# Edge rows turned behind the last tile, layer 0's sums cleared by ScalarE, packed words unpacked the other way round

## The reference

```
x = LN(x + relu(GAT(x)))            # layer 0: 8 heads, softmax over the edges of a node
x = LN(x + two GCN convolutions)    # layer 1: 256 -> 512 -> 256, degree norms, layer norms, relu
x = LN(x + relu(segsum((x@W)[src] * edge_weight, dst) + b))          # layer 2
m = (x@Wf.T)[src]*attr0 + (x@Wr.T)[src]*attr1                        # layer 3: 4 heads
x = LN(x + segsum(softmax(leaky(m@a.T)) * m, dst))
```

## Time and profile before

| | before |
|---|---|
| device time, median of 3 runs | 6573.53 us (6570.21 to 6581.08) |
| span of the profiled execution, first to last instruction | 5313.9 us |
| mean granted TensorE clock | 0.820 |
| busy: PE, DVE, ACT, POOL | 74%, 66%, 48%, 73% |

### The profile page before, as it was taken

How to read it: one execution, slowest core, us unless ns; L and a number is a source line. 1 busy time by engine, 2 the same in 40 slices (tenths; PEclk the granted TensorE clock), 3 DMA queues, 4 the chain that set the end, 5 groups by cost and what they waited for, 6 DMA issues and landing times.

```text
span 5313.9 us, 86764 instructions
## 1 busy us (share of the span) xinstructions
PE 3931.6 (74%) x13357; PEld 2389.2 (45%) x13357; DVE 3517.2 (66%) x10780; ACT 2554.6 (48%) x6938; POOL 3875.0 (73%) x3995
## 2 busy tenths in 40 slices
PE   6888888887777777677777777777677656666763
PEld 4666666664444444344444443343333333444442
DVE  6789888885554545444444445666666578888887
ACT  1667667664555555455545552000000166666665
POOL 3777777775777777677777776777777677777775
PEclk8889889988899998887777777877888777777776
DMA  5444444443333333443333333333333322222222
GB/s 151 113 122 126 122 126 124 120 121 98 111 112 112 111 112 111 118 139 111 111 112 112 111 112 100 109 109 109 109 108 109 98 57 57 57 57 57 57 57 68
DMA packets 252628, 549.14 MB, mean 103 GB/s; under 512 B 71467, under 2 KB 136235, under 8 KB 252108
## 3 DMA queue, kind: packets, MB, share of 16 engines
q0 software_dynamic: 178752, 478.34, 32.8%
q1 hardware_dynamic: 66972, 58.64, 3.5%
q10 hardware_dynamic: 6384, 6.62, 0.5%
HBM read 501.16 MB, written 42.15 MB: 102 GB/s over the span
## 4 chain that ended last, share of the span: by engine, by line
PE 32%; POOL 22%; DMA 18%; issue 13%; DVE 6%; ACT 6%; SPq 2%; DVEq 1%; ACTq 0%; POOLq 0%
PE bank L1453 18%; POOL scratch L1863 12%; DMA scratch<-tab_x,src_idx 10%; POOL scratch L1399 9%; DMA scratch<-tab_h,src_idx 7%; PE bank L1297 4%; PE bank L172 4%; PE bank L1154 3%; DVE reg_acc L1463 2%; ACT scratch L1066 2%; POOL reg_x L1024 2%; SPq L865 1%; DVE reg_acc L1322 1%; PE bank L1142 1%; PE bank L157 1%
## 5 line engine op out<-in xcount | busy, mean ns | idle before, releaser
L1453 PE MATMUL bank<-scratch 128*128 x4986 | 1946.5, 501 | 739.9 <-SPq L1414 356.6
L1463 DVE TENSOR_TENSOR reg_acc<-reg_acc,bank 128x256 f32 x2493 | 1047.3, 420 | 1368.2 <-PE bank L1453 1310.3
L1399 POOL DMA_INDIRECT scratch<-tab_x,src_idx x1566 | 1494.3, 954 | 533.5 <-issue 259.4
L1453 PEld LDWEIGHTS bank<-scratch 128*128 128x128 f32 x4986 | 961.2, 229 | 1630.2 <-issue 1582.6
L1024 POOL DMA_INDIRECT reg_x<-tab_h,src_idx x832 | 838.7, 1008 | 302.7 <-issue 184.1
L1399 POOL DMA_INDIRECT scratch<-tab_h,src_idx x783 | 746.6, 953 | 264.7 <-issue 153.0
L1863 POOL DMA_INDIRECT scratch<-tab_h,src_idx x783 | 743.0, 949 | 249.3 <-issue 226.8
L1916 PE MATMUL bank<-reg_w,scratch 128*128 128x260 f32 x1664 | 639.8, 527 | 282.7 <-issue 180.1
L1423 ACT ACTIVATE scratch<-iota_row,dst_loc 128x128 f32<-128x128 f32 x1662 | 579.6, 393 | 345.5 <-PE bank L1453 336.1
L1297 PE MATMUL bank<-reg_x,scratch 128*128 128x265 f32 x1664 | 582.4, 461 | 72.7 <-DVE reg_x L1339 70.4
L1916 PEld LDWEIGHTS bank<-reg_w,scratch 128*128 128x128 f32 x1664 | 376.3, 252 | 505.1 <-issue 305.0
(11 more groups left out here) (313 smaller groups left out, 4364.1 us busy)
## 6 DMA issues: line engine op xcount, KB each, us to landing
scratch<-tab_x,src_idx POOLq DMA_INDIRECT x1566, 2.8
scratch<-tab_h,src_idx POOLq DMA_INDIRECT x1566, 2.7
reg_x<-tab_h,src_idx POOLq DMA_INDIRECT x832
tab_h<-scratch ACTq DMA_DIRECT2D x7, 924.0 KB, 5.2
reg_x<-in_x SPq DMA_DIRECT2D x7, 896.0 KB, 11.3
reg_w<-in_x SPq DMA_DIRECT2D x49, 128.0 KB, 2.3
tab_x<-reg_acc SPq DMA_DIRECT2D x49, 128.0 KB
tab_xs<-reg_w SPq DMA_DIRECT2D x49, 128.0 KB, 2.6
```

Of the source, the lines that this page charges most:

```text
L1399: e.indirect_dma_start(ring_rows[:, j % SLOTS, :], None, self.table, bass.IndirectOffsetOnAxis(ap=src_idx[:, j:j + 1], axis=0)).then_inc(* ...
L1453: e.matmul(self.bank(i), ring_hots[:, i % HOTS, :], rows, start=True, stop=True).then_inc(*self.product.up)
L1463: e.tensor_tensor(v, v, self.bank(i), ALU.add).then_inc(*self.added.up)
```

## The change

Four edits.

1. The preparation handles one source row at each of the steps 28 to 34, and nothing more until step `LATER_PIECE` = 54, behind the last tile. From there on it handles four of the other 42 rows at a step. `FLAGS` moves from step 53 to step 65.
2. DVE's memset of 13,312 columns goes. ACT clears the same columns by copying a column of zeros: columns 2200 to 9855 as soon as all edge rows are kept, and columns 0 to 2199 and 9856 to 13311 behind `prep_over`, ahead of its part of the chain. DVE's first addition of layer 0 waits for the last of these copies. DVE writes the column of zeros at the start.
3. The word is turned round: `slot * 256 * 1024 + position + 1`. The count is now masked (1023) and the slot is shifted (10). In the steps on PE and ACT the count is taken first, then the slot.
4. `steps_through`, SP's value of its wait in the mix stage, is masked with 1023 before it is copied.

```diff
-PLACES = 2 ** 16
+PLACE_BITS = 10
+PLACES = 2 ** PLACE_BITS
...
-        FLAGS = FIRST_PIECE + -(-len(EDGE_ROWS) // 2)
+        LATER_PIECE = NODE_TILES + 5
+        FLAGS = LATER_PIECE + -(-(len(EDGE_ROWS) - STEP_BLOCKS) // 4)
 
         def piece(i):
 
-            n = i - FIRST_PIECE
-            return range(2 * n, min(2 * n + 2, len(EDGE_ROWS))) if n >= 0 else ()
+            first, later = i - FIRST_PIECE, STEP_BLOCKS + 4 * (i - LATER_PIECE)
+            if i >= LATER_PIECE:
+                return range(later, min(later + 4, len(EDGE_ROWS)))
+            return range(first, first + 1) if inside(first, STEP_BLOCKS) else ()
...
-                e.tensor_scalar(landed_of, position, 1.0, float(PLACES), ALU.add,
-                                ALU.mult).then_inc(*pre_v.done("landed_of"))
+                e.tensor_scalar(landed_of, position, 1.0, None, ALU.add).then_inc(*pre_v.done("landed_of"))
                 e.wait_ge(*pre_v.at("landed_of"))
-                e.scalar_tensor_tensor(out=slot_i, in0=slot_of, scalar=float(FEAT), in1=landed_of, op0=ALU.mult,
+                e.scalar_tensor_tensor(out=slot_i, in0=slot_of, scalar=float(FEAT * PLACES), in1=landed_of, op0=ALU.mult,
...
+            e.memset(zeros, 0.0).then_inc(*pre_v.done("zeros"))
...
         def slot_rows(e, name, t, a, b):
             words, parts = slot_regs[name]
-            e.reg_alu(parts[0], words[t % GROUP], PLACES - 1, op=ALU.bitwise_and)
+            e.reg_alu(parts[0], words[t % GROUP], PLACE_BITS, op=ALU.logical_shift_right)
...
         def chunks_needed(e, name, t):
             words, parts = slot_regs[name]
-            e.reg_alu(parts[1], words[t % GROUP], 16, op=ALU.logical_shift_right)
+            e.reg_alu(parts[1], words[t % GROUP], PLACES - 1, op=ALU.bitwise_and)
...
         def steps_through(e, c):
-            return e.snap(end_regs[c % ENDS_AT_ONCE], min_val=1, max_val=STEPS)
+            e.reg_alu(end_regs[ENDS_AT_ONCE], end_regs[c % ENDS_AT_ONCE], PLACES - 1, op=ALU.bitwise_and)
+            return e.snap(end_regs[ENDS_AT_ONCE], min_val=1, max_val=STEPS)
...
+        def clear(e, a, b):
+            return e.copy(reg_acc[:, a:b], zeros.to_broadcast([P, b - a]))
+
         def heads_scalar(e):
+            e.wait_ge(*pre_v.at("zeros"))
+            e.wait_ge(*row_kept.end)
+            clear(e, at_kept, at_flags).then_inc(*h0_a.done("middle_clear"))
             prep_over(e)
+            clear(e, 0, at_kept).then_inc(*h0_a.done("start_clear"))
+            clear(e, at_flags, at_rest).then_inc(*h0_a.done("end_clear"))
...
-            e.wait_ge(*pre_p.at("rest_clear"))
-            e.memset(reg_acc[:, 0:at_rest], 0.0).then_inc(*h0_v.done("clear"))
             e.tensor_scalar(src_at, src_at_i, turn_by, None, ALU.add).then_inc(*h0_v.done("src_less"))
...
             for k in range(S):
                 chain_vector(e, 0, k)
+            e.wait_ge(*pre_p.at("rest_clear"))
+            e.wait_ge(*h0_a.at("end_clear"))
             for i in range(STEPS_PAD):
...
-                rows, needed = slot_rows(e, "tensor", i, 0, FEAT), chunks_needed(e, "tensor", i)
+                needed = chunks_needed(e, "tensor", i)
+                rows = slot_rows(e, "tensor", i, 0, FEAT)
```

More of the change, by code:

```diff
@@ L309, in build @@
         sums = acc[:, :, 0:FEAT]
-        eps_col = small[:, 440:441]
+        eps_col, zeros = small[:, 440:441], small[:, 442:443]
         rings_a = reg_b[:, 6700:6840]
@@ L397, in build @@
         at_flags = STEP_BLOCKS * (2 * NI + NF) * P
-        at_rest = at_flags + 128 + 4 * STEPS_PAD
+        at_rest, at_kept = at_flags + 128 + 4 * STEPS_PAD, 2200
         ints = reg_acc[:, 0:at_flts].bitcast(I32).rearrange("p (b f) -> p b f", b=STEP_BLOCKS)
@@ L422, in build @@
         pre_v = v_order.named(
-            "iota_row part ident step_no ones_row end_tile end_f ones_wide line prod_src w_src prod_dst w_dst "
+            "iota_row part ident step_no ones_row zeros end_tile end_f ones_wide line prod_src w_src prod_dst w_dst "
             "ends first_less first next_all next key_part of_tile key up_and_next diag most_key is_most "
@@ L429, in build @@
             "ranks1 closed groups through0 through1 "
-            + " ".join(f"src{b}" for b in range(STEP_BLOCKS)) + " " + " ".join(f"dst{b}" for b in range(STEP_BLOCKS)) +
-            " adst flag valid cap start_flag start_mask end_flag end_mask counts ones_col run0 run1 run2 run3 heads "
+            + " ".join(f"src{b}" for b in range(STEP_BLOCKS)) + " adst " + " ".join(f"dst{b}" for b in range(STEP_BLOCKS)) +
+            " flag valid cap start_flag start_mask end_flag end_mask counts ones_col run0 run1 run2 run3 heads "
             "low_starts low_ends goes_on goes_valid going going_less carried eps")
@@ L863, in load_ends @@
             if not end_regs:
-                end_regs.extend(e.alloc_register(f"end{k}") for k in range(ENDS_AT_ONCE))
+                end_regs.extend(e.alloc_register(f"end{k}") for k in range(ENDS_AT_ONCE + 1))
             e.load(end_regs[0:n], ends_row[0:1, c0:c0 + n])
         def steps_through(e, c):
-            return e.snap(end_regs[c % ENDS_AT_ONCE], min_val=1, max_val=STEPS)
+            e.reg_alu(end_regs[ENDS_AT_ONCE], end_regs[c % ENDS_AT_ONCE], PLACES - 1, op=ALU.bitwise_and)
+            return e.snap(end_regs[ENDS_AT_ONCE], min_val=1, max_val=STEPS)
         def rank_value(e, name, t):
@@ L900, in build @@
         bank_t, bank_3, bank_d, bank_c = (psum[4], psum[5]), psum[6][:, 0:3 * P], psum[6][:, 3 * P:4 * P], psum[7]
-        h0_v = v_order.named("level begins ones clear src_less src_below src_at")
+        h0_a = a_order.named("middle_clear start_clear end_clear")
+        h0_v = v_order.named("level begins ones src_less src_below src_at")
         h0_p = p_order.named("src_idx")
@@ L1941, in turn_about @@
                     load_slots(e, "scalar", i)
-                row, needed = slot_rows(e, "scalar", i, SIDE3, ROW3), chunks_needed(e, "scalar", i)
+                needed = chunks_needed(e, "scalar", i)
+                row = slot_rows(e, "scalar", i, SIDE3, ROW3)
                 e.wait_ge(s_landed[3].sem, needed)
```

## The result

| | before | after |
|---|---|---|
| median of 4 runs each | 6571.87 us (6553.84 to 6581.08) | 6504.49 us (6498.42 to 6513.4) |
| ratio, 95% interval | | 0.9907 (0.9881 to 0.9934) |
| span of the profiled execution | 5313.9 us | 6500.7 us |
| that execution's own time | not listed | 6502.46 us |
| mean granted TensorE clock | 0.820 | 0.734 |

67 us less by the medians, 61 by the ratio, where 22 were forecast. The second half of the table matters more. So next to nothing lies around a span, and the trace from which the prediction was read, 1260 us shorter than the runs, was of an execution in another condition of the hardware. On chips 5 and 9 the kernel before takes 5311 to 5316 us, on chips 3 and 7 it takes 6562 to 6641.

A forecast was written before the change was run, and what follows sets the result against it. POOL's gather queue was taken to set the pace nearly everywhere, except in the preparation. Starting 10.5 us earlier and losing a 13.2 us stall, less 1.5 for crowding, with 0 for the words, gave -22: 6551.5 us (6541 to 6560; all cases 6537 to 6575).

The forecast's parts named there:

- Which condition the trace shows: Around the profiled span: 1259.6 us at the median taken to lie outside it and stay unchanged.
- The words: Register steps on PE, ACT, DVE and SP: 0 us, hidden; DVE's mix-stage bounds -33 to +31 us.
- The tiles: Preparation: last store of `tab_h0` 10.5 us earlier, so POOL's first gather of layer 0 at 87.1 instead of 97.61.
- The stall: Layer 0's 14.12 us gather: DVE's memset blamed for keeping POOL from writing descriptors; removing it saves 13.2 us.
- rival C: Layer 0: the long gather has another cause and stays; 9.5 us gained, 6564 us; chance 0.07.
- The rows behind the tiles and the clears: Preparation: `eps` 4 us later at 114.7, ACT's two clears 4.2 us, line 1114 at about 122 instead of 135.21.
- Layer 0's end: Layer 0 ends 22 us earlier and everything behind moves equally; first gather of layer 1 at about 1214.
- rival B: Layer 0: the chain never catches up with POOL, so it ends only 13 us earlier; 6560.5 us; chance 0.22.
- Rival D: Mix stage: SP's added instruction per position costs 51 us if its queue is the pace; 6602.5 us; chance 0.05.
- The preparation: Preparation and start of layer 0: earlier POOL start and removed memset stall, less crowding, together 22 us less.
- rival E: Behind layer 0: the gain is there but doesn't reach the end; about 6571 us; chance 0.14.

The follow-up runs named there:

- all_3: Whole change, all four edits, against the kernel before, on chip 5: 5292.51 us against 5310.74, ratio 0.9965.
- words_3: Kernel before with only the turned word and SP's mask (edits 3 and 4), on chip 5: 5313.4 us, ratio 1.0003 to the kernel before.
- dve_more_2: Edits 3 and 4 alone plus one more mask on DVE in each mix-stage step, on chip 3: 6648.65 us, ratio 1.0017 to the kernel before.
- dve_arith: Edits 3 and 4 alone, but DVE's slot taken by arithmetic shift (ALU_OP and MOVE, the form of before), on chip 5: 5309.01 us, ratio 1.0 to the kernel before.
- words_clears: Kernel before with edits 3 and 4 plus ACT's clears replacing DVE's memset, on chip 7: 6519.21 us, ratio 0.9935 to the kernel before.
- words: Kernel before with only edits 3 and 4 (turned word, SP's mask), on chip 7: 6523.53 us against 6561.85, ratio 0.9941.
- all_2: Whole change, all four edits, against the kernel before, on chip 3: 6573.95 us against 6641.45, ratio 0.9895.
- words_rows_2: Kernel before with edits 3 and 4 plus the later edge rows (edit 1), DVE's memset kept, on chip 3: 6581.43 us, ratio 0.991 to the kernel before.
- after: The changed kernel's first measurement, all four edits, against the kernel before: 6504.49 us against 6571.87, ratio 0.9907.

## Why the prediction was right or wrong

**Which condition the trace shows: wrong, and the root of the rest.** The prediction noted that the span stood 1259.6 us below the median and wrote: "What lies around the span, 1259.6 us at the median, I take as unchanged". No such part exists: a span is 1.8 us below its execution's time. The 1260 us lie inside the stages, most of them as silences of all engines. Measured by what an added instruction costs there, DVE's queue is part of the pace in the mix stage and PE's in two passes.

**The words: wrong, and the term that was mis-sized.** The prediction wrote of DVE: "I take 0, since DVE is busy 678 of 790 us there and POOL's 1.25 us a gather is the pace". On chips 5 and 9 that is right to within 0.1% in seven kernels besides `all_3`, with fewer instructions and with more. In the timed condition a gather comes each 1.55 us in the mix stage:

```profile
L1878 POOL DMA_INDIRECT scratch<-tab_h,src_idx x783: 938/944/1137, 5135.3 to 6344.6; - x196
```

The cover by POOL is gone there. Measured for all of the words: -38 us on chip 7 (-25 to -52), where the term was 0. The bounds of -33 to +31 were DVE's alone, and the measured time doesn't tell DVE's part from PE's.

The prediction priced DVE's term by the durations of the instructions and gave their number no price. The trace has one fused instruction for the mask and the copy of before, and it is longer than both: 122 ns against 40 + 36. That is 46 ns more a step, beyond the +37 that was the upper bound, and 38 us more in DVE's queue over 832 steps. On a calm chip the stage gets no longer by it (978.1 us from first to last gather in `words_3`, 980.4 before).

What one instruction less is worth on a slow chip can only be estimated. On chip 3 the stage grows by 46 / 1664 = 28 ns for each further instruction on DVE, and by 27 / 831 = 32 and 31 / 831 = 38 ns for PE's MOVE in the second and third pass, one a step. Applied to the change, DVE's one instruction less in 832 steps would be 832 x 28 = 23 us of the 38. Another way to estimate it gives less: by `dve_more_2` an ALU_OP and the MOVE take 91 + 86 = 177 ns on the mean where the fused one takes 145, so 27 us of queue, and at the 46 us of stage for 104 of queue that is 12. Neither is a measurement: the kernel before was not traced on such a chip, and its own form (`dve_arith`) ran only on calm ones. So 15 to 26 us of the 38 stay open. PE and ACT have as many instructions as before, of the same kinds, in another order.

**The tiles: right.** The first gather was forecast for 87.1 and found at 85.41 on chip 5, 12 us earlier than before's 97.61 (11 than `words_3`'s 96.4). On chips 7 and 3 it is 10 to 15 us earlier with edit 1 than without.

**The stall: right as a mechanism, its worth not shown.** The long gather went with the memset and moved with it, so rival C is refuted. What its 13.2 us are worth in the end was measured only on slow chips: 4 us (`words_clears` against `words`) and 7.5 (`all_2` against `words_rows_2`). On chip 5 the clears were not run without the rows.

**The rows behind the tiles and the clears: right.** `eps` was forecast for 114.7 and found at 115.44. The two clears took 5.0 us, not 4.2, and ACT's chain copy came at 120.65, not 119.2. Line 1114's instruction was forecast for "about 122" and stands at 122.79; DVE's readiness for about 118, and it is 118.25; group 1's chain for 139, and it is 139.51.

**Layer 0's end: nearly right.** The last gather starts at 1169.2 us, 19.2 ahead of before's 1188.4, where 22 were forecast. It isn't B's 13, though the interval of `all_3`'s ratio, 12 to 25 us, would still admit that. The first gather of layer 1 was forecast for 1214 and stands at 1224.2. The way from layer 0's last gather to it took 55 us in this execution, against 48 in before's and 43 to 53 in the seven kernels of chip 5 without edits 1 and 2, and the traced execution was the slow one of its kernel, 12 us above the median. By the prediction's own sign, a first gather near 1223 means rival B. The row of the last gather speaks against it (the seven have 1186.2 to 1193.3 there), and the time of the runs, 18.6 us, lies between the two. B's smaller gain isn't excluded.

**Rival D: the mechanism is real, the engine and the sign were wrong.** It had register work decide the mix stage, by SP's added mask, at +30. The count of DVE's and PE's instructions decided, and the time went down. SP's mask, doubled, costs nothing on chips 5 and 9 (1.0006 and 0.9998). POOL waits 278.7 us for SP's queue in the changed kernel's trace, so what it costs on a slow chip is open.

**The sum.** The preparation was forecast at -22 and measured at -18.6 on chip 5, and on chip 7 at -14.5 by the medians and -18 by the ratios; it reached the end, so rival E is out. The words were forecast at 0 and measured at -38. On chip 7 the two are -53 by the medians and -56 by the ratio; the first measurement has -61 by its ratio (43 to 78 by its interval). That the words carry 38 of it is shown; that the register instructions' number is why is shown for added ones and argued for the change itself.

## What to carry to other kernels

Compare the span of the profiled execution with the timed runs before reading anything else. If they differ by more than some microseconds, the trace is probably of another condition, and what it calls the pace, and what it shows as hidden, needn't hold in the runs. Where sequencers pause, count register instructions and not only their nanoseconds in a calm trace: one fused instruction instead of two is worth trying on a queue that is near the pace, even if it is longer than the two. And move a long memset of DVE away from POOL's gathers, or give it to ACT.

## What was unexpected of the hardware

- The same kernel takes 5311 to 5316 us on two chips and 6562 to 6641 us on two others, each steady within 0.7%. On the slow ones DVE's 128x256 addition (420 ns) and POOL's gather (0.95 us) are as long as ever. The matmuls are longer on the mean (516 ns in `after` against 498 in `all_3` in the passes, 581 against 532 in the mix stage), and the granted TensorE clock is 0.73 where it was 0.82. The register instructions that unpack the words are some 20 to 110 ns longer on the mean, in pauses of up to 1.4 us; those of layer 0 aren't. What causes the pauses stays open.
- Register instructions whose medians have the same sum are not of the same price there: 122 ns in one piece and 126 ns in three differ by 46 us over 832 steps. On the calm chips they don't differ (0.9994).
- A memset without any SBUF input, 11.15 us long, holds up a POOL gather until 1.24 us behind its end, though the gather started 1.7 to 2.7 us ahead of it.
